# Language-model tower on one core: place of the embedding gathers on GpSimd, and the queue that issues the rows of all maxima

## The chip, the cores and the metric

The kernel runs on one core of a Trainium2 chip. The metric is the device time of one execution in microseconds, median of several. Engines are TensorE (PE), VectorE (DVE), ScalarE (ACT), GpSimd (POOL) and SyncE (SP); SPq in a profile row is SP's sequencer issuing DMAs.

## What is computed

```python
h = embeddings[x]                                  # x: 8 batches x 256 tokens, embeddings 8000 x 256, all float32
n = layernorm(h)
q, k, v = heads(n @ w_qkv)                         # 16 heads of 16
q, k = rotary(q), rotary(k)
h = h + (softmax(q @ k.T / 4) @ v).merge_heads() @ w_proj
n = layernorm(h)
e = argmax(n @ gate_w.T)                           # one of 8 experts per token
out = h + n + n @ expert_w[e].T
```

## The kernel before, in words

The work is cut into 8 batches (`NB`) of 256 tokens, each as two tiles (`NT`) of 128 rows. Each engine has its own program, written out by hand: a prologue, then `steps(step)`, which runs steps b = -1 to 9 of 16 slots s each. In step b TensorE computes for batch b the scores a second time, now turned and with the maximum already taken off (tile `t_pair`, `t_scores_tile`), ScalarE turns them into `probs` (`exp`), and TensorE multiplies those with the values into `o_bank`. In the same step the scores of batch b+1 are computed for the first time (tile `s_pair`, `scores_tile`), and VectorE takes their row maxima (`neg_max`, L857). So step -1 holds only first scores of batch 0, and step 0 is the first with second scores. Beside these the steps hold the front of a later batch (layer norm, QKV product, rotation, transposes, value product) by the tables `FRONT`, `EARLY`, `ONE` and `TWO`, the rest of attention of batch b-1 (`POST`), and the eight experts of batch b-2 in `e_bank`.

Exact float32 products come from float32r pairs: a high part, copied by ScalarE (`qk_high`, `x_high`, ...), and a low part, made by VectorE (`qk_low`, L849, and others).

Three things matter for the change.

**Gathers.** `gather(b)` on GpSimd issues two indirect DMAs (L325), each fetching 128 embedding rows into `h0` for one tile. VectorE's `f_norm_a(b)` (BN_STATS on `h0`, L811) waits for `gathered[b]`. GpSimd then computes the reciprocal deviation (`f_rs_of`, L335 and L337), VectorE normalizes (`xn`, L823), and TensorE transposes `xn` (L438) into the QKV product. In the prologue of GpSimd `gather(2)` stands behind the two rotation sums of batch 0 (`rotated_sum`, tile `qk`, L342), which wait for products of batch 0. `gather(3)` ends the prologue, and `gather(4)` to `gather(7)` stand at slot 6 of steps -1 and 0, where nothing else of GpSimd lies between.

**Restacking.** `restack(b)` on SP moves the rotated, transposed q and k parts into the operand layout `stacks`: six DMAs of 256 KB from SBUF to SBUF (L280). TensorE's first scores of batch b wait for all of them (`stack_in`).

**Rows of all maxima.** When the maxima of eight heads of a batch are complete, VectorE splits them (L864, L866), TensorE transposes them (L502), ScalarE copies the 16 rows to `max_rows` (`max_row`, L696), and SP issues two DMAs of 8 KB (`maximum(b, u)`, L267) which put them as two more operand rows into `stacks`. The second scores wait for them (`m_in[u]`, at v = 0 and v = 4). SP's order in a step is: maxima (b, 1), restack of b+2, maxima (b+1, 0), store of b-2. Each waits in order.

Of the kernel before, what the change touches and what calls it, by code (L numbers as in the profile page):

```python
# [7 lines left out]
F32 = mybir.dt.float32  # L8
# [12 lines left out]
STACKS = 3  # L21
# [14 lines left out]
def tower(nc, x, emb, w_qkv, w_proj, gate_w, expert_w, rope, ramp, out):  # L36
# [12 lines left out]
    with ExitStack() as ctx:  # L49
# [197 lines left out]
        @block.sync  # L247
        def _(sp):
            sp.sem_inc(out_ok, 16)
            sp.dma_start(ids[:, :], x).then_inc(ids_in, 16)  # L250
            for c in range(C):
                sp.dma_start(wqkv_raw[:, c, :], w_qkv[c * P:(c + 1) * P, :]).then_inc(wqkv_in[c], 16)
            sp.dma_start(rope_sb[:, :, :, :], rope).then_inc(rope_in, 16)
            sp.dma_start(ramp_sb[:, :], ramp).then_inc(rope_in, 16)
            sp.dma_start(gw_raw[:, :, :], gate_w).then_inc(gw_in, 16)

            for b in range(2):
                sp.wait_ge(gathered[b], 16 * NT)
            sp.dma_start(wp_raw, w_proj.rearrange("(c p) n -> p c n", p=P)).then_inc(wp_in, 16)
            sp.dma_start(ew_raw[:, :, :], expert_w).then_inc(ew_in, 16)  # L260

            def maximum(b, u):

                wait(sp, mt_ok, b * 2 + u + 1)
                for half in range(2):
                    r = 64 * half + KS
                    sp.dma_start(stacks[b % STACKS][r:r + 2, 4 * u:4 * u + 4, 0, :].bitcast(F32),  # L267
                                 max_rows[8 * half:8 * half + 8, u, :].bitcast(F32)).then_inc(m_in[u], 16)

            def restack(b):  # L270

                wait(sp, qkh_ok, b * NT + NT)
                wait(sp, t_ps, (b - STACKS) * NH + NH)
                for i in range(3):
                    if i == 1:
                        wait(sp, again_ok, b * NT + NT)
                        wait(sp, qkl_ok, b * NT + NT)
                    for half in range(2):
                        r = 64 * half
                        sp.dma_start(stacks[b % STACKS][r + i:r + KS:3, :, :, :].bitcast(F32).rearrange("d j k n -> d j (k n)"),  # L280
                                     parts[:, half, 2 * i:2 * i + 2, :].bitcast(F32)).then_inc(stack_in, 16)

            def store(b):
                wait(sp, res_ok, b + 2)
                sp.dma_start(out[b].rearrange("(t p) d -> p t d", p=P), res[:, :, :]).then_inc(out_ok, 16)

            def step(b, p):
                if here(b, 0):
                    maximum(b, 1)
                if here(b, 2):  # L290
                    restack(b + 2)
                if here(b, 1):
                    maximum(b + 1, 0)
                if here(b, -2):
                    store(b - 2)


            sp.wait_ge(ones_ok, 1)
            def ones_rows(i):
                for half in range(2):  # L300
                    r = 64 * half + KS
                    sp.dma_start(stacks[i][r:r + 2, :, 1, :].bitcast(F32), ones[:, :]).then_inc(ones_in, 16)

            for i in range(STACKS):
                ones_rows(i)
            restack(0)
            steps(step)
            sp.wait_ge(out_ok, 16 * (NB + 1))


        @block.gpsimd
        def _(pool):
# [61 lines left out]
            def step(b, p):  # L374
                for s in range(SLOTS):
                    g_at = SLOTS * b + s
                    for t in range(NT):
                        for k in batches(front, f"rotate{t}", g_at):
                            rotated_sum(k, t)
                    for k in batches(front, "stats", g_at):  # L380
                        f_rs_of(k)
                    for k in batches(post, "stats", g_at):
                        g_rs_of(k)
                    for k in batches(post, "g_norm", g_at):
                        residuals(k)
                    if s == 0 and here(b, -3):
                        finish(b - 3)
                    if s == 6 and b in (-1, 0):
                        gather(2 * b + 6)
                        gather(2 * b + 7)  # L390
                    if s % 2 and b == 1:
                        expert_weights([s // 2])
                if b == NB + 1:
                    finish(b - 2)
# [2 lines left out]
                gather_tile(j)  # L397
            f_rs_of(0)
            gather_tile(3)
            f_rs_of(1)  # L400
            rotated_sum(0, 0)
            rotated_sum(0, 1)
            gather(2)
            f_rs_of(2)
            rotated_sum(1, 0)
            rotated_sum(1, 1)
            gate_weights()
            rotated_sum(2, 0)
            rotated_sum(2, 1)
            gather(3)  # L410
            steps(step)


# [280 lines left out]
        def _(act):  # L694
# [22 lines left out]
            def max_row(b, u):  # L717
                wait(act, mt_ps, b * 2 + u + 1)
                copy(max_rows[:, u, :], o_bank[0:16, N:2 * N]).then_inc(mt_ok, 1)

            def exp(b, v):
                if v % 2 == 0:
# [331 lines left out]
```

## Time and profile before

| quantity | value |
|---|---|
| time, median of 3 runs | 328.38 us (328.08 to 330.29) |
| time of the profiled execution | 331.04 us |
| its span, first to last instruction | 329.2 us |
| busy share of the span | TensorE 86%, VectorE 74%, ScalarE 39%, GpSimd 26% |
| one step in the middle (step 3) | 33.5 us |
| prologue and step -1 together, until the first second scores | 58.7 us |

A timeline row has start and duration in us, then engine, line, operation, tiles, and in brackets how long the engine sat idle before and what ended that. A row of "windows" has the stretch and its length, then the busy time of each engine with its number of instructions, the granted TensorE clock (1.00 is 2.4 GHz, 0.50 is 1.2 GHz), the share of time that the 16 DMA engines were busy, and GB/s.

### The profile page before, as it was taken

The page shows a single profiled execution, that of the slowest core. Times are in us where ns is not written, and L with a number is a line of the kernel's source. Part 1 is how long each engine was busy: PE and PEld are TensorE (multiplying, and loading weights), DVE is VectorE, ACT ScalarE, POOL GpSimd, SP SyncE. Part 2 cuts the span into 40 slices and gives each one's busy share as a digit, 9 for nine tenths or more (in the row PEclk, how much of TensorE's full clock was granted, in tenths as well). Part 3 has the DMA queues.
Part 4 walks back from the last instruction along what each step waited for, and adds up shares of the span by engine and source line. Part 5 has one row for each costly group of instructions (what it writes and reads, how often), then busy time and mean ns, then how long its engine had stood idle before and what let it go on. Part 6 is the DMA issues. An engine that isn't in the chain of part 4 may idle for free.

```text
span 329.2 us, 5465 instructions
## 1 busy us (share of the span) xinstructions
PE 282.2 (86%) x2000; PEld 202.1 (61%) x2000; DVE 243.6 (74%) x595; ACT 126.9 (39%) x261; POOL 85.1 (26%) x96
## 2 busy tenths in 40 slices
PE   0384866789788899998999899989999999999894
PEld 0263744545565577667766677667666766667582
DVE  5764477565789887988798779877887985557763
ACT  3041030633596354435443544354454353431100
POOL 4551476011257601231122112220210120120311
PEclk9999675555999999999999999999999999999999
DMA  3269059093048029002900191019200000000000
GB/s 113 68 248 181 10 98 138 0 144 53 1 82 115 2 54 141 5 0 59 157 16 1 44 166 22 0 36 162 35 32 4 0 4 34 3 1 34 0 32 32
DMA packets 11590, 19.14 MB, mean 58 GB/s; under 512 B 2012, under 2 KB 4903, under 8 KB 11436
## 3 DMA queue, kind: packets, MB, share of 16 engines
q1 hardware_dynamic: 10796, 18.24, 29.1%
q0 software_dynamic: 768, 0.55, 1.2%
q8 instruction: 16, 0.26, 0.4%
q14 instruction: 10, 0.08, 0.1%
HBM read 5.30 MB, written 2.10 MB: 22 GB/s over the span
## 4 chain that ended last, share of the span: by engine, by line
PE 46%; DVE 25%; issue 11%; POOL 7%; DMA 5%; ACT 3%; SPq 1%; POOLq 0%; DVEq 0%; ACTq 0%
PE e_bank L424 13%; PE o_bank L554 7%; PE f_bank L424 7%; DVE acc L936 5%; PE t_pair L519 5%; DVE neg_max L857 5%; POOL qk L342 4%; DMA h<-in_emb,ids 2%; PE s_pair L424 2%; DMA stacks<-max_rows 2%; PE m_bank L566 2%; PE m_bank L424 2%; POOL res L360 2%; PE s_pair L490 1%; DVE xn L823 1%
## 5 line engine op out<-in xcount | busy, mean ns | idle before, releaser
L726 ACT ACTIVATE probs<-t_pair 128x512 f32<-128x512 f32 x128 | 69.6, 596 | 95.3 <-PE t_pair L519 94.8
L857 DVE TENSOR_REDUCE neg_max<-s_pair 128x2 f32<-128x512 f32 x128 | 81.9, 682 | 17.0 <-PE s_pair L490 16.4
L490 PE MATMUL s_pair<-stacks 48*128 48x256 f32 x256 | 55.8, 343 | 3.6 <-DVE neg_max L857 3.3
L519 PE MATMUL t_pair<-stacks 50*128 50x256 f32 x256 | 50.1, 326 | 5.4 <-DMA stacks<-max_rows 3.7
L519 PEld LDWEIGHTS t_pair<-stacks 50*128 50x128 f32 x256 | 35.9, 201 | 28.1 <-issue 25.1
L424 PE MATMUL e_bank<-ew_h,y_h 128*128 128x512 f32 x92 | 40.4, 439 | 4.7 <-DVE acc L932 2.7
L490 PEld LDWEIGHTS s_pair<-stacks 48*128 48x128 f32 x256 | 40.0, 213 | 6.3 <-DVE neg_max L857 5.1
L554 PE MATMUL o_bank<-probs,vals 128*32 128x256 f32 x512 | 36.9, 408 | 1.2 <-ACT max_rows L696 1.2
L936 DVE SCALAR_TENSOR_TENSOR acc<-e_bank,mask,acc 128x256 f32<-128x256 f32 x66 | 28.8, 478 | 11.2 <-PE e_bank L424 10.7
L424 PE MATMUL e_bank<-ew_l,y_h 128*128 128x512 f32 x92 | 36.3, 395 | 0.0
L424 PE MATMUL e_bank<-ew_h,y_l 128*128 128x512 f32 x92 | 36.3, 395 | 0.0
L342 POOL TENSOR_TENSOR qk<-rope_a,rope_b 128x512 f32<-128x512 f32 x16 | 20.7, 1294 | 49.0 <-DVE rope_b L844 49.0
L424 PEld LDWEIGHTS e_bank<-ew_h,y_h 128*128 128x128 f32 x92 | 17.3, 188 | 12.0 <-DVE acc L936 3.9
L554 PEld LDWEIGHTS o_bank<-probs,vals 128*32 128x32 f32 x512 | 14.0, 113 | 14.9 <-issue 7.5
L424 PE MATMUL f_bank<-wqkv_h,x_h 128*128 128x512 f32 (+1 forms) x44 | 17.7, 402 | 3.5 <-DVE x_l L828 2.6
L424 PEld LDWEIGHTS e_bank<-ew_l,y_h 128*128 128x128 f32 x92 | 17.3, 188 | 4.2
L335 POOL TENSOR_SCALAR f_ve<-f_mv 128x2 f32<-128x2 f32 x8 | 2.4, 295 | 67.3 <-DVE f_mv L814 67.3
L349 POOL TENSOR_SCALAR g_ve<-g_mv 128x2 f32<-128x2 f32 x8 | 2.0, 246 | 68.0 <-DVE g_mv L814 68.0
L696 ACT ACTIVATE o_t<-o_bank 128x256 f32<-128x256 f32 x32 | 12.5, 390 | 16.1 <-PE o_bank L554 16.1
L424 PEld LDWEIGHTS e_bank<-ew_h,y_l 128*128 128x128 f32 x92 | 17.4, 189 | 2.1
L325 POOL DMA_INDIRECT h<-in_emb,ids x16 | 16.8, 1048 | 6.1 <-issue 3.9
L360 POOL TENSOR_TENSOR res<-acc 128x512 f32<-128x512 f32 x8 | 10.2, 1276 | 31.0 <-DVE acc L936 31.0
(132 smaller groups left out, 529.8 us busy)
## 6 DMA issues: line engine op xcount, KB each, us to landing
stacks<-parts SPq DMA_DIRECT2D x48, 256.0 KB
ew_raw<-in_expert_w SPq DMA_DIRECT2D x1, 2048.0 KB, 9.2
out<-res SPq DMA_DIRECT2D x8, 256.0 KB, 2.1
probs<-in_w_qkv SPq DMA_DIRECT2D x2, 384.0 KB, 3.5
stacks<-max_rows SPq DMA_DIRECT2D x32, 8.0 KB
h<-in_emb,ids POOLq DMA_INDIRECT x16, 4.7
probs<-in_w_proj SPq DMA_DIRECT2D x1, 256.0 KB, 2.8
stacks<-ones SPq DMA_DIRECT2D x6, 16.0 KB
```

Source lines behind the costliest of these rows:

```text
L325: g.indirect_dma_start(h0[:, j, :], None, emb, bass.IndirectOffsetOnAxis(ap=ids[:, j:j + 1], axis=0), bounds_check=V - 1, oob_is_err=False ...
L342: g.tensor_tensor(qk[:, t, :, :, :].rearrange("p g d j -> p g j d"), rope_a[:, t, :, :].rearrange("p (g j) d -> p g j d", j=8), rope_b[:, ...
L360: g.tensor_tensor(res[:, :, :], acc[:, 0, :, :], acc[:, 1, :, :], ALU.add).then_inc(res_ok, 1)
L424: m = mm(o, a(c), w(c), start=(n == 0), stop=(n == 3 * C - 1))
L490: m = mm(s_pair[:, half, t * N:(t + 1) * N], stacks[b % STACKS][r:r + KS, pair, 0, t * P:(t + 1) * P], stacks[b % STACKS][r:r + KS, pair, ...
L519: m = mm(t_pair[:, half, c * N:(c + 1) * N], stacks[b % STACKS][r:r + KM, pair, 1, c * P:(c + 1) * P], stacks[b % STACKS][r:r + KM, pair, ...
L554: m = mm(o_bank[STRIP * j:STRIP * (j + 1), 0:N], vals[b % VALS][:, c, head(4 * g + j), :], probs[:, (4 * g + j) % RING, c, :], start=(c == ...
L566: m = tr(strips_bank(b, t)[:, g * P:(g + 1) * P], o_t[:, g, t * P:(t + 1) * P], ident[:, :])
L696: return nc.scalar.activation(o, i, ACT.Copy)
L726: nc.scalar.activation(probs[:, (2 * v + half) % RING, :, :].rearrange("p c n -> p (c n)"), t_pair[:, half, :], ACT.Exp, scale=SCALE).then ...
L857: v.tensor_reduce(neg_max[:, k // 4, :, 4 * half + k % 4], s_pair[:, half, :].rearrange("p (t n) -> p t n", t=NT), AX.X, ALU.max, negate=T ...
L936: v.scalar_tensor_tensor(out=acc[:, j, t, :], in0=y, scalar=mask[:, p, t, e:e + 1], in1=base[:, t, :] if u == 0 else acc[:, j, t, :], op0= ...
```

## The change

On GpSimd, `gather(2)` is issued right behind `gather_tile(3)` in the prologue, ahead of `f_rs_of(1)` and of the rotation sums of batch 0. `gather(3)` to `gather(7)` are issued one per step, at slot 1 of steps 0 to 4. The function `maximum` of SP is gone; its two DMAs are issued by ScalarE at the end of `max_row`, behind a wait for the copy that writes their source.

```diff
--- SP
-            def maximum(b, u):
-                wait(sp, mt_ok, b * 2 + u + 1)
-                for half in range(2):
-                    r = 64 * half + KS
-                    sp.dma_start(stacks[b % STACKS][r:r + 2, 4 * u:4 * u + 4, 0, :].bitcast(F32),
-                                 max_rows[8 * half:8 * half + 8, u, :].bitcast(F32)).then_inc(m_in[u], 16)
             def step(b, p):
-                if here(b, 0):
-                    maximum(b, 1)
                 if here(b, 2):
                     restack(b + 2)
-                if here(b, 1):
-                    maximum(b + 1, 0)
                 if here(b, -2):
                     store(b - 2)
--- POOL
-                    if s == 6 and b in (-1, 0):
-                        gather(2 * b + 6)
-                        gather(2 * b + 7)
+                    if s == 1 and b >= 0 and here(b, 3):
+                        gather(b + 3)
...
             gather_tile(3)
+            gather(2)
             f_rs_of(1)
             rotated_sum(0, 0)
             rotated_sum(0, 1)
-            gather(2)
             f_rs_of(2)
...
             rotated_sum(2, 1)
-            gather(3)
             steps(step)
--- ACT
             def max_row(b, u):
                 wait(act, mt_ps, b * 2 + u + 1)
                 copy(max_rows[:, u, :], o_bank[0:16, N:2 * N]).then_inc(mt_ok, 1)
+                wait(act, mt_ok, b * 2 + u + 1)
+                for half in range(2):
+                    r = 64 * half + KS
+                    act.dma_start(stacks[b % STACKS][r:r + 2, 4 * u:4 * u + 4, 0, :].bitcast(F32),
+                                  max_rows[8 * half:8 * half + 8, u, :].bitcast(F32)).then_inc(m_in[u], 16)
```

GpSimd's program from the first gathers on, before the change (L325 is a gather of one tile, L335 and L337 the deviation, L342 a rotation sum, L371 the gate weights, L366 expert weights):

```order
L325 DMA h<-in_emb,ids 128x256 x3
L335 TENSOR_SCALAR f_ve<-f_mv 128x2
L337 TENSOR_TENSOR f_rs<-f_ve,neg_half 128x2
L325 DMA h<-in_emb,ids 128x256
L335 TENSOR_SCALAR f_ve<-f_mv 128x2
L337 TENSOR_TENSOR f_rs<-f_ve,neg_half 128x2
L342 TENSOR_TENSOR qk<-rope_a,rope_b 128x4x8x16 x2
L325 DMA h<-in_emb,ids 128x256 x2
L335 TENSOR_SCALAR f_ve<-f_mv 128x2
L337 TENSOR_TENSOR f_rs<-f_ve,neg_half 128x2
```

The same place after the change (a gather is now L313, the deviation L323 and L325, a rotation sum L330):

```order
L313 DMA h<-in_emb,ids 128x256 x3
L323 TENSOR_SCALAR f_ve<-f_mv 128x2
L325 TENSOR_TENSOR f_rs<-f_ve,neg_half 128x2
L313 DMA h<-in_emb,ids 128x256 x3
L323 TENSOR_SCALAR f_ve<-f_mv 128x2
L325 TENSOR_TENSOR f_rs<-f_ve,neg_half 128x2
L330 TENSOR_TENSOR qk<-rope_a,rope_b 128x4x8x16 x2
L323 TENSOR_SCALAR f_ve<-f_mv 128x2
L325 TENSOR_TENSOR f_rs<-f_ve,neg_half 128x2
```

The two gathers of batch 2 have moved up past the deviation of batch 1 and both rotation sums of batch 0. Behind the last rotation sum of the prologue ten gathers in a row (batches 3 to 7) have become two (batch 3).

ScalarE's program in step 3, from the copy of the transposed q and k high part of tile 0, before (L726 is the exponential, L696 every copy):

```order
L696 ACTIVATE parts<-f_bank 128x2x2x128
L726 ACTIVATE probs<-t_pair 128x512 x2
L696 ACTIVATE parts<-parts 128x2x2x128
L696 ACTIVATE max_rows<-o_bank 16x256
L696 ACTIVATE parts<-f_bank 128x2x2x128
L726 ACTIVATE probs<-t_pair 128x512 x2
```

The same place after (copies are L682, exponentials L717, the DMAs L709):

```order
L682 ACTIVATE parts<-f_bank 128x2x2x128
L717 ACTIVATE probs<-t_pair 128x512 x2
L682 ACTIVATE parts<-parts 128x2x2x128
L682 ACTIVATE max_rows<-o_bank 16x256
L709 DMA stacks<-max_rows 2x4x256 x2
L682 ACTIVATE parts<-f_bank 128x2x2x128
L717 ACTIVATE probs<-t_pair 128x512 x2
```

Two DMA issues stand behind each of the 16 copies of maxima. On SP the 32 issues are gone, so that the restack of a batch no longer stands behind the maxima of the step.

## Rows read from the trace of the kernel before

**Rows 1.** The page: TensorE's granted clock in 40 slices, 8.2 us each

```profile
PEclk9999675555999999999999999999999999999999
```

**Rows 2.** The page: the chain that ended last, shares of the span by line

```profile
PE e_bank L424 13%; PE o_bank L554 7%; PE f_bank L424 7%; DVE acc L936 5%; PE t_pair L519 5%; DVE neg_max L857 5%; POOL qk L342 4%; DMA h<-in_emb,ids 2%; PE s_pair L424 2%; DMA stacks<-max_rows 2%; PE m_bank L566 2%; PE m_bank L424 2%; POOL res L360 2%; PE s_pair L490 1%; DVE xn L823 1%
```

**Rows 3.** Windows: steps 1 and 3

```profile
83.00:116.50 33.50, 28.05 (x251) 19.17 (x251) 28.53 (x66) 21.45 (x46) 17.17 (x16) 1.00 0.32 49
...
150.20:183.70 33.50, 32.22 (x251) 23.51 (x251) 28.49 (x73) 14.72 (x32) 7.05 (x8) 1.00 0.32 58
```

**Rows 4.** Timeline of GpSimd: the gather of tile 3, the gathers of batch 2

```profile
11.05 1.27 POOL L325 DMA_INDIRECT h<-in_emb,ids  x1 [0.19 <-issue]
15.20 0.22 POOL L335 TENSOR_SCALAR f_ve<-f_mv 128x2 f32<-128x2 f32 x1 [2.88 <-DVE f_mv L814]
...
21.78 1.14 POOL L325 DMA_INDIRECT h<-in_emb,ids  x1 [0.15 <-issue]
23.22 1.00 POOL L325 DMA_INDIRECT h<-in_emb,ids  x1 [0.30 <-issue]
```

**Rows 5.** Timeline of VectorE: moments of batch 1, low weights, statistics of batch 2

```profile
14.80 0.30 DVE L814 BATCH_NORM_AGGREGATE f_mv<-f_st 128x2 f32<-128x6 f32 x2
...
24.62 0.69 DVE L941 TENSOR_TENSOR wp_l<-probs,wp_h 128x512 fp32r<-128x512 f32 x1 [0.63 <-issue]
28.32 0.75 DVE L811 BATCH_NORM_STATS2 f_st<-h 128x6 f32<-128x256 f32 x2 [3.00 <-DMA h<-in_emb,ids]
```

**Rows 6.** Timeline of TensorE: transpose of batch 2

```profile
31.32 1.05 PE L438 MATMUL m_bank<-ident,xn 128*128 128x128 f32 x4 [3.57 <-DVE xn L823]
```

**Rows 7.** Windows of one microsecond: DMA after the expert weights, clock at 31 us

```profile
21.00:22.00 1.00, 0.47 (x5) 0.26 (x4) 0.09 (x1) 0.73 (x3) 0.85 (x2) 1.00 0.22 82
...
31.00:32.00 1.00, 0.68 (x4) 0.67 (x4) 1.00 (x3) 0.00 (x0) 0.00 (x0) 0.69 1.08 180
```

**Rows 8.** The chain: six products of batch 2, at half and at full clock

```profile
36.21 2.37 PE f_bank L424 x6
38.58 1.40 PE e_bank L424 x6
```

**Rows 9.** Windows: the restacks of batches 1, 2 and 3 in flight

```profile
45.00:57.00 12.00, 8.57 (x27) 6.10 (x26) 9.59 (x19) 0.37 (x1) 8.25 (x9) 0.50 1.09 155
...
67.00:77.00 10.00, 8.65 (x62) 5.36 (x54) 6.36 (x16) 5.21 (x12) 0.94 (x2) 0.50 1.03 158
...
95.00:105.00 10.00, 7.84 (x77) 5.62 (x74) 9.41 (x25) 7.49 (x16) 6.35 (x9) 1.00 1.02 157
```

**Rows 10.** The chain at the end of step -1, and TensorE's first second score

```profile
51.70 6.64 DMA stacks<-max_rows
...
58.69 0.55 PE L519 MATMUL t_pair<-stacks 50*128 50x256 f32 x1 [3.66 <-DMA stacks<-max_rows]
```

**Rows 11.** Timeline of VectorE: the last maxima of batch 0

```profile
54.48 1.29 DVE L857 TENSOR_REDUCE neg_max<-s_pair 128x2 f32<-128x512 f32 x2 [0.29 <-PE s_pair L490]
```

**Rows 12.** Line L267: duration in ns (min/median/max), first and last start

```profile
L267 SPq DMA_DIRECT2D stacks<-max_rows x32: 610/616/664, 51.0 to 274.8; - x32
```

**Rows 13.** The page: DMA issues of the output store, median us to landing

```profile
out<-res SPq DMA_DIRECT2D x8, 256.0 KB, 2.1
```

**Rows 14.** Timeline of ScalarE around the copy of maxima, steps 1 and 3

```profile
92.28 0.36 ACT L696 ACTIVATE max_rows<-o_bank 16x256 fp32r<-16x256 f32 x1
92.91 0.60 ACT L696 ACTIVATE vals<-f_bank 128x512 f32<-128x512 f32 x1 [0.27 <-PE f_bank L424]
...
96.83 0.62 ACT L696 ACTIVATE o_h<-m_bank 128x512 fp32r<-128x512 f32 x1
...
152.91 0.60 ACT L696 ACTIVATE parts<-f_bank 128x512 fp32r<-128x512 f32 x1
```

**Rows 15.** Step 3: VectorE's low part of tile 1, TensorE's value product

```profile
153.54 0.69 DVE L849 TENSOR_TENSOR parts<-f_bank,parts 128x512 fp32r<-128x512 f32 x1
...
155.37 0.28 PE L424 MATMUL f_bank<-wqkv_h,x_h 128*128 128x256 f32 x1
```

## The prediction

> **What bounds the kernel now.** I read the page first. TensorE's granted clock is full except in a stretch of slices near 33 us and from about 41 to 82 us [rows 1]. The chain that ended last is mostly TensorE and VectorE work, but it holds two DMA entries of 2% each, the gather into `h` and the rows of all maxima; 2% of 329.2 us is 6.6 us for each [rows 2]. Then I read windows by step. Step 3 has TensorE busy 32.22 of 33.5 us: there it is the bound and only about 1.3 us are free. Step 1 has 28.05 of 33.5 us, because expert work has not begun; it is bound by a chain over several engines and has ScalarE at 21.45 us instead of 14.72 us, since it also splits the expert weights there [rows 3]. Last I looked at the two places where a DMA entry of the chain becomes idle time. In the prologue VectorE sits idle for 3.00 us until the gather of batch 2 lands at 28.3 us, and TensorE then waits 3.57 us for the normalized batch 2 [rows 5, 6]. At the start of step 0 TensorE waits 3.66 us for the rows of all maxima of batch 0, whose DMA is in flight for 6.64 us, until 58.34 us [rows 10]. Nothing else of the two topics shows as a wait on the path, so the change can give only at these two places, plus what the granted clock adds.
>
> **Gather of batch 2, earlier.** It is issued at 21.78 and 23.22 us now, behind two rotation sums. In the new order it follows the gather of tile 3, which ends at 11.05 + 1.27 = 12.32 us. Two issues at the durations and gaps of the present pair (0.15 + 1.14 + 0.30 + 1.00 = 2.59 us) end at 14.9 us [rows 4]. The next GpSimd instruction, the deviation of batch 1, waits until 15.1 us for VectorE's moments in any case (14.80 + 0.30) [rows 5] and stands idle for 2.88 us before it [rows 4]. So the two issues lie in that hole and cost nothing; if they took 0.5 us longer, the excess would fall on batch 1 alone, which has its own slack behind batch 0. The landing: the last gather was issued at 23.22 us and landed at 28.3 us, 5.1 us later, in company of the first restack. Now the expert weights are in flight beside it, and the DMA engines have fallen to a share of 0.22 by 21 to 22 us [rows 7], so it has landed by 22 us at the latest. VectorE reaches its statistics only behind the low part of the projection weights, which ends at 24.62 + 0.69, overlapped to about 25.25 us [rows 5]. Gain: 28.32 - 25.25 = 3.05 us. All behind it (deviation, `xn`, transposes, the rotation of batch 1, the product of batch 2) hangs on this one instruction in VectorE's order and moves up by the same amount. VectorE's own order is late next, not the DMA. Bounds: 3.05 us if the weights stay where they are; 2.5 us if the two issues delay batch 1's path a little.
>
> TensorE's idle time ahead of this transpose shrinks from 3.57 to 0.5 us, and a second, shorter hole behind it, the wait for the rotation sum of batch 1, stays. The granted clock fell to 0.69 at 31 us and then to 0.50, behind the 3.57 us hole [rows 7]. If it stayed full, the six products of batch 2 behind it would be about 1.0 us shorter (2.37 us against 1.40 us for six at either clock [rows 8]). But it is reduced again from the slice of 41 to 49 us on [rows 1], where TensorE has no hole as long as that one, so I count this at zero and keep 1.0 us for the range.
>
> **Later gathers, one per step.** The eight gathers of batches 4 to 7 leave the stretch in which the restack of batch 1 is in flight (45 to 57 us, in which GpSimd runs nine gathers in 8.25 us). With them that restack keeps the DMA engines busy for 12 us (45 to 57 us). The restacks of batches 2 and 3, same size, no gathers, need 10 us each [rows 9]. I take the difference, about 2.2 us since the two gathers of batch 3 stay: the restack lands near 55.0 us on the old time axis instead of 57.2 us, where the 12 us end. At their new places, slot 1 of a step, GpSimd has 17.17 and 7.05 us of work in 33.5 us [rows 3]; each pair costs 2.6 us there, is needed seven slots (some 14 us) later, and delays nothing but a first piece of expert weights in step 1, needed in step 2. Cost: nothing.
>
> **Rows of all maxima, on ScalarE's queue: what it brings.** ScalarE's copy is its only instruction between 45 and 57 us [rows 9], so it can issue when SP did, from 51.0 us [rows 12], ending at about 52.3 us. Until now the two DMAs queued behind 1.5 MB of restack on the same queue and landed 6.64 us after the issue [rows 10]. On another queue they are only beside it. Bounds for the landing: 2 us after the issue (2.1 us, the landing of a store [rows 13]) is 54.3 us; all the way behind the restack, which itself now lands at 55.0 us, is 56.1 us. I take 55.3 us. But the first visit of step 0 also waits for the restack of batch 1 (55.0 us) and for the maxima of batch 0, of which the first half is ready at 54.48 + 0.65 = 55.1 us and the rest at 54.48 + 1.29 = 55.8 us [rows 11]. So three waits end almost together, and TensorE starts at about 55.8 us instead of 58.69 us. Gain 2.9 us, between 2.1 (behind the restack) and 3.5 us (only the maxima left). What is late next is VectorE.
>
> The Trainium skill bears on this in two places. "Trainium Kernel Development and Optimization", section Key Constraints, says that DMAs of all queues share the same 16 engines and that a second issuer only saves the sequencer's issue time; by that the queue brings nothing, and this term would be the 2.2 us from the gathers alone, 0.7 us less. "DMA: Bandwidth & Descriptors", section on queues and rings, says that an engine takes turns between the queues that it has work for, by which the small rows pass the restack. The 6.64 us flight is what one shared queue looks like; no row here shows two hardware queues at once.
>
> **What it costs.** Sixteen copies are each followed by two issues that now stand in ScalarE's order. On SP one takes 616 ns [rows 12]; I take the same, so 2 x 0.64 + 0.05 = 1.3 us per copy, 21 us of ScalarE time in all. Not measured on ScalarE: the low bound is nothing, the high one 1.6 us. Most of it falls into waits for TensorE. Where not:
> - Step 1. ScalarE has 0.27 us of idle time behind the copy at 92.28 us, then runs values, expert weights, exponentials and `o_h` (96.83 us) with no gap worth the name [rows 14]. So `o_h` comes 1.3 - 0.3 = 1.0 us late, and the chain of step 1 runs through it (out projection, residual, norm). TensorE is not the bound there [rows 3], so the 1.0 us stays. The second copy of step 1 is followed by a wait for TensorE, and I cost it at nothing.
> - Steps 2 to 5. The high part of tile 1 follows the copy at once (152.91 us) [rows 14]. It moves to 154.2, the low part on VectorE from 153.54 to 154.8, ending 155.5, and TensorE's value product (155.37 us) waits for it [rows 15]: 0.2 us late. Four such steps at 0.1 to 0.2 us: 0.6 us. VectorE's order then carries 1.3 us, which it gives back in its next wait for TensorE: it is free for 5 of 33.5 us [rows 3].
> - The copy of the next batch's maxima at slot 11: exponentials and `y_h` come 1.3 us later, and their readers stand behind a whole expert product in TensorE's order, 1.4 us at full clock as six products of that size are [rows 8]. Nothing.
> Sum of costs 1.6 us, bounds 0 and 3.7 us (if the steps in the middle pay 0.7 us each).
>
> Taking SP out of the maxima lets the restack go a little earlier; it is not waited for in any step but 0, so nothing.
>
> **The sum.** -3.05 - 2.9 + 1.6 = -4.35 us. The profiled execution took 331.04 us (span 329.2 us and 1.84 us around it), so it would become 326.7 us. It was 2.66 us above the median of the runs; the same difference on the median gives 328.38 - 4.35 = 324.0 us.
>
> **Rivals.**
> - *The wait only changes its name.* The restack of batch 1 keeps 12 us of flight, because bandwidth inside SBUF, not the gathers, sets it (155 GB/s with gathers, 158 and 157 without [rows 9] would fit that). TensorE then waits for `stack_in` until about 57.9 us, gain 0.7 instead of 2.9 us: 326.2 us. Against it stands the recorded time, 2 us more at nearly the same rate. By the section Key Constraints named above the time would be 324.7 us.
> - *The clock.* With the prologue's hole gone and the one at 55 us gone, the granted clock stays or returns to full earlier. From 49 to 82 us it was at half [rows 1]. Keeping it in the prologue gives 1.0 us, a return 3 us earlier in step 0, where TensorE is busy for 8.65 of 10 us at that clock [rows 9], another 1.5 us: 321.5 us.
> - *ScalarE's queue becomes the bound.* The place is `max_row`: a stalled issue holds back exponentials, which hold back TensorE's second scores and the outputs. At 1.3 us in full for all 16 copies it is 20.8 us against a gain of 5.95 us: 328.38 + 14.9 = 343 us. It decides from 0.37 us of loss per copy on (5.95 / 16), and is slower by over 1% from 0.58 us on. For it: ScalarE must wait for its own copy each time, and the maxima sit in front of exponentials. Against it: ScalarE is idle for more than half of every step [rows 3].
> - *Not what it says.* A gather of batch 2 that lands after 25.25 us because of the expert weights; excluded by rows 7 but for an unknown.
>
> **Chances.** The forecast 0.50, with its own range 322.6 to 325.5 us. Clock 0.17. Wait renamed 0.13. ScalarE's cost at two to three times my figure, near 326 us, 0.13. ScalarE as the bound 0.07. A change of 1%, 3.3 us, is about what a measurement of this kernel can tell from none. Below 325.1 us lie most of the forecast and all of the clock case: 0.62. Within 1%: 0.31. Slower by over 1%: 0.07. The range goes from 320.5 us (-3.05, -3.5, no cost, clock 1.0, rounded) to 328.0 us (gains of 3.05 and 0.7, cost 3.7).
>
> **What would show it.** Right, if VectorE's statistics of batch 2 start near 25.25 us with no wait for a DMA; if the first second score starts 5 to 6.5 us earlier than 58.69 us, its wait ended by VectorE or by a DMA landing within half a microsecond of it; if the stretch of busy DMA engines of that restack is 10 us; if ScalarE's queue rows last about 0.6 us; if step 1 is some 1 us longer and step 3 at most 0.3 us. Wrong, if that first visit still waits for the restack, if steps 2 to 5 grow by over 0.7 us each, or if the granted clock has another shape.

## The result, and the profile after

The changed kernel takes 335.9 us, the median of 5 runs (334.23 to 336.18), against 328.4 us (328.08 to 330.29): ratio 1.020, 95% interval 1.0173 to 1.0228. It is slower by 7.5 us where 4.35 us of gain were forecast, and lies outside the range. The profiled execution took 334.23 us with a span of 332.4 us, 3.2 us more than the span of before. Executions of one kernel differ here by 2 to 6 us with their mean granted clock, so the ratios leave out executions of the slower kind where a kernel showed both (three of seven for gathers alone, four of nine for held until landed, one of eight for held until copied, four of ten for both queues), and the traces are compared place by place.

First the page of the changed kernel: the granted clock in 40 slices and the chain that ended last, by line.

```profile
PEclk9999765659798999999999999999999999999999
...
PE e_bank L410 14%; PE f_bank L410 6%; PE o_bank L540 6%; DMA stacks<-max_rows 6%; DVE acc L927 4%; PE t_pair L505 4%; DVE neg_max L848 4%; PE m_bank L410 3%; ACTq L709 3%; ACT parts L682 3%; POOL qk L330 2%; ACT probs L717 2%; PE s_pair L410 2%; PE s_pair L476 2%; POOL res L348 2%
```

The gather into `h` has left the chain [rows 2], as intended. The rows of all maxima have not: they have grown from 2% to 6%, and a new entry, ScalarE's queue (ACTq L709), has 3%. TensorE's waits, from the list of who waited for whom (total, times, longest), show the same:

```profile
PE t_pair L505 <- DMA stacks<-max_rows: 8.8, 3, 4.0
```

One wait of 3.66 us [rows 10] has become three. Where they stand, in TensorE's timeline of the changed kernel:

```profile
55.09 0.55 PE L505 MATMUL t_pair<-stacks 50*128 50x256 f32 x1 [2.13 <-DMA stacks<-max_rows]
...
68.88 0.58 PE L505 MATMUL t_pair<-stacks 50*128 50x256 f32 x1 [3.97 <-DMA stacks<-max_rows]
...
97.73 0.38 PE L505 MATMUL t_pair<-stacks 50*128 50x256 f32 x1 [2.70 <-DMA stacks<-max_rows]
```

The first is the old one: the first second score is at 55.09 instead of 58.69 us, 3.6 us earlier. The other two stand in front of the fifth pair of heads (v = 4) of steps 0 and 1, where no DMA was waited for before. They are for the rows of (b, 1), the second half of the heads.

A clock for the whole run are ScalarE's 16 copies of maxima (start in us; the last columns are the difference to before). The versions are those of the experiments below.

| copy of | before | changed | changed - before | gathers alone - before | held - before |
|---|---|---|---|---|---|
| (0, 0) | 50.59 | 48.52 | -2.07 | -2.26 | -2.45 |
| (0, 1) | 64.16 | 60.52 | -3.64 | -3.64 | -3.87 |
| (1, 0) | 71.04 | 70.74 | -0.30 | -3.65 | -3.87 |
| (1, 1) | 92.28 | 90.06 | -2.22 | -4.17 | -4.66 |
| (2, 0) | 100.08 | 101.31 | +1.23 | -4.17 | -2.45 |
| (2, 1) | 118.54 | 120.65 | +2.11 | -4.19 | -0.03 |
| (3, 1) | 152.47 | 154.56 | +2.09 | -4.18 | -0.02 |
| (4, 1) | 185.94 | 188.41 | +2.47 | -4.19 | +0.34 |
| (5, 1) | 219.41 | 222.24 | +2.83 | -4.19 | +0.69 |
| (7, 1) | 273.75 | 276.93 | +3.18 | -4.16 | +1.09 |

So the changed kernel is 3.64 us ahead until the copy of (0, 1). It loses 3.34 us at the first new wait and regains 1.92 us in step 0. In step 1 it loses 3.45 us up to the copy of (2, 0), a stretch that holds the second new wait but also two issues on ScalarE, and 0.88 us more behind that copy; then 3 x 0.36 us in steps 3 to 5. The sum is +3.19 us. The regain is clock: the granted clock is at full for slices of step 0 in which it was at half before [rows 1].

The prologue, in GpSimd's and VectorE's timelines, answers to [rows 4, 5]:

```profile
12.37 1.01 POOL L313 DMA_INDIRECT h<-in_emb,ids  x1 [0.30 <-issue]
13.68 1.01 POOL L313 DMA_INDIRECT h<-in_emb,ids  x1 [0.30 <-issue]
15.14 0.22 POOL L323 TENSOR_SCALAR f_ve<-f_mv 128x2 f32<-128x2 f32 x1 [0.45 <-DVE f_mv L805]
```

```profile
19.80 0.69 DVE L831 TENSOR_TENSOR rope_a<-e_bank,rope_sb 128x512 f32<-128x512 f32 x1 [1.20 <-PE e_bank L410]
...
25.55 0.69 DVE L932 TENSOR_TENSOR wp_l<-probs,wp_h 128x512 fp32r<-128x512 f32 x1 [0.46 <-ACT wp_h L682]
26.15 0.75 DVE L802 BATCH_NORM_STATS2 f_st<-h 128x6 f32<-128x256 f32 x2
```

Both gathers lie in GpSimd's hole, and the statistics of batch 2 follow the low weights at once, with no wait for a DMA. They start at 26.15 instead of 28.32 us.

The new mechanism is in SP's and ScalarE's queues. In step 0, from the chain (the flight is counted from the start of the second of the two issues):

```profile
60.91 0.62 ACTq L709
61.57 7.27 DMA stacks<-max_rows
68.84 0.04 issue
```

The rows of (0, 1) were in flight for 7.27 us. What was on the DMA engines then, queue by queue (packets, MB, share of 16 engines; q1 is SP's, q10 ScalarE's), in the stretches 60 to 62, 62 to 64, 64 to 66 and 66 to 68 us:

```profile
q1 hardware_dynamic: 197, 0.37, 84.6%
...
q1 hardware_dynamic: 157, 0.29, 105.9%
...
q1 hardware_dynamic: 159, 0.29, 100.0%
q10 hardware_dynamic: 10, 0.01, 3.8%
...
q1 hardware_dynamic: 173, 0.32, 102.5%
q10 hardware_dynamic: 10, 0.01, 3.9%
```

SP's queue is the restack of batch 2, 1.5 MB. SP began to issue it at 59.18 us, 1.7 us before the rows were issued. In the kernel before, SP issued the rows of (b, 1) first and could not reach the restack of b+2 until they were out. With the rows gone from SP, the restack starts as soon as its parts are ready, which in steps 0 and 1 is before the copy of (b, 1) (tables `TWO` and `EARLY`: transposes in slots 0 and 1, the copy in slot 3). The 20 packets of the rows then move 10 by 10, the first of them more than 3 us after their issue. From step 2 on the second transpose stands in slot 3 behind the copy, so the restack can't overtake, and no wait appears.

### The profile page after: what moved, and what is told of

The parts are those of the page before. It is cut to its first block, busy times and chain, and to the rows that moved or that the text cites. A ratio compares the mean times of both kernels' runs of the same rounds, so it can differ in the third digit from the quotient of the medians.

```text
span 332.4 us, 5465 instructions
## 1 busy us (share of the span) xinstructions
PE 282.8 (85%) x2000; PEld 201.8 (61%) x2000; DVE 244.0 (73%) x595; ACT 127.0 (38%) x261; POOL 85.5 (26%) x96
## 4 chain that ended last, share of the span: by engine, by line
PE 44%; DVE 20%; issue 11%; ACT 8%; DMA 7%; POOL 6%; ACTq 3%; POOLq 0%; DVEq 0%
PE e_bank L410 14%; PE f_bank L410 6%; PE o_bank L540 6%; DMA stacks<-max_rows 6%; DVE acc L927 4%; PE t_pair L505 4%; DVE neg_max L848 4%; PE m_bank L410 3%; ACTq L709 3%; ACT parts L682 3%; POOL qk L330 2%; ACT probs L717 2%; PE s_pair L410 2%; PE s_pair L476 2%; POOL res L348 2%
## 5 line engine op out<-in xcount | busy, mean ns | idle before, releaser
L717 ACT ACTIVATE probs<-t_pair 128x512 f32<-128x512 f32 x128 | 69.7, 597 | 95.1 <-PE t_pair L505 86.3
L330 POOL TENSOR_TENSOR qk<-rope_a,rope_b 128x512 f32<-128x512 f32 x16 | 20.6, 1293 | 50.8 <-DVE rope_b L835 50.8
L337 POOL TENSOR_SCALAR g_ve<-g_mv 128x2 f32<-128x2 f32 x8 | 2.0, 244 | 68.2 <-DVE g_mv L805 68.2
L323 POOL TENSOR_SCALAR f_ve<-f_mv 128x2 f32<-128x2 f32 x8 | 2.4, 297 | 66.1 <-DVE f_mv L805 66.1
L682 ACT ACTIVATE o_t<-o_bank 128x256 f32<-128x256 f32 x32 | 12.5, 390 | 16.8 <-PE o_bank L540 13.7
L313 POOL DMA_INDIRECT h<-in_emb,ids x16 | 17.1, 1070 | 5.5 <-issue 3.4
```

The costliest lines, as they stand in the source:

```text
L313: g.indirect_dma_start(h0[:, j, :], None, emb, bass.IndirectOffsetOnAxis(ap=ids[:, j:j + 1], axis=0), bounds_check=V - 1, oob_is_err=False ...
L330: g.tensor_tensor(qk[:, t, :, :, :].rearrange("p g d j -> p g j d"), rope_a[:, t, :, :].rearrange("p (g j) d -> p g j d", j=8), rope_b[:, ...
L682: return nc.scalar.activation(o, i, ACT.Copy)
L717: nc.scalar.activation(probs[:, (2 * v + half) % RING, :, :].rearrange("p c n -> p (c n)"), t_pair[:, half, :], ACT.Exp, scale=SCALE).then ...
```

## The experiments

Times are medians in us over all executions; "before" is the kernel before, run beside them.

| run | time | before | ratio to before (95%) |
|---|---|---|---|
| gathers alone | 322.9 | 328.95 | 0.978 (0.974 to 0.982) |
| the same again | 324.92 | 328.59 | 0.987 (0.9825 to 0.9916) |
| rows on ScalarE alone | 340.22 | 328.95 | 1.033 (1.0289 to 1.037) |
| changed, restack held until rows landed | 331.36 | 328.95 | 1.0001 (0.9955 to 1.0046) |
| changed, restack held until rows copied | 332.34 | 328.95 | 1.0092 (1.0057 to 1.0127) |
| gather of batch 2 alone | 326.15 | 329.52 | 0.9918 (0.9889 to 0.9946) |
| later gathers alone | 329.04 | 329.52 | 0.9981 (0.9951 to 1.0011) |
| held, issues one slot later | 326.28 | 329.52 | 0.9866 (0.979 to 0.9941) |
| rows on both queues | 327.44 | 329.52 | 0.9883 (0.9835 to 0.9931) |
| gathers, SP's order swapped | 368.37 | 328.59 | 1.1207 (1.1169 to 1.1245) |
| changed, issues one slot later, not held | 337.17 | 328.59 | 1.0232 (1.0176 to 1.0287) |

**Each half alone.** The first run keeps `maximum` on SP and takes only the gathers from the change.

```diff
             def step(b, p):
                 if here(b, 0):
                     maximum(b, 1)
                 if here(b, 2):
                     restack(b + 2)
                 if here(b, 1):
                     maximum(b + 1, 0)
```

> Both moves of the gathers, maxima still issued by SP in the old order. Theory (the restack overtakes the maxima rows only because SP no longer stands between them): the first second score starts near 55.1 us, no wait of TensorE for maxima rows at v = 4 of steps 0 and 1, steps 3 to 5 at 33.5 us; time 328.4 - 3.6 = about 324.8 us. Rival (the moved gathers bring a loss of their own in steps 0 and 1, for instance by meeting the restacks): the waits in front of the second scores of v = 4 appear here too and the time is 328 us or more.

TensorE's timeline of this version:

```profile
55.05 0.55 PE L517 MATMUL t_pair<-stacks 50*128 50x256 f32 x1 [2.29 <-DMA stacks<-max_rows]
```

That is the only wait for rows left in its timeline of TensorE. The lead of 3.64 us holds through step 0, grows by 0.5 us with the clock, and is 4.2 us to the end (table). The rival falls. The row says one thing more: the first second score comes at 55.05 us with the rows on SP's queue and at 55.09 us on ScalarE's. The own queue brought nothing there. The seven executions lie between 321.45 and 326.9 us, and the ratio of 0.978 comes from four at a mean granted clock of 0.957 or more, so it was run again.

> The version with the gather moves alone, once more in five rounds: 322 to 327 us depending on the granted clock in the first 100 us, ratio to the kernel before 0.98 to 0.99. The version with both repairs of ScalarE's issues should not differ from it by more than 1 us at the same granted clock.

The second time six executions of 322.92 to 327.4 us gave 0.987, which is the better figure for this version, since all six count in it.

The other half: gathers as before, rows on ScalarE.

```diff
                 copy(max_rows[:, u, :], o_bank[0:16, N:2 * N]).then_inc(mt_ok, 1)
+                wait(act, mt_ok, b * 2 + u + 1)
+                for half in range(2):
+                    r = 64 * half + KS
+                    act.dma_start(stacks[b % STACKS][r:r + 2, 4 * u:4 * u + 4, 0, :].bitcast(F32),
+                                  max_rows[8 * half:8 * half + 8, u, :].bitcast(F32)).then_inc(m_in[u], 16)
```

> Only the issue of the maxima rows moved to ScalarE, gathers as before. Theory: first second score hardly earlier than 58.69 us (0 to 0.7 us), then the two waits for maxima rows of the changed kernel (3.3 and 3.5 us of lost lead), less what the granted clock gives back in step 0, 0.9 us in step 1 and 3 x 0.36 us in steps 3 to 5; time 334 to 337 us. Rival (the two edits meet badly and neither is bad alone): 328 to 330 us.

TensorE's timeline, steps 0 and 1:

```profile
72.69 0.58 PE L507 MATMUL t_pair<-stacks 50*128 50x256 f32 x1 [5.00 <-DMA stacks<-max_rows]
...
103.22 0.38 PE L507 MATMUL t_pair<-stacks 50*128 50x256 f32 x1 [2.82 <-DMA stacks<-max_rows]
```

340.22 us, more than the 334 to 337 us expected; the first new wait is 5.00 us here instead of 3.97 us. The first second score starts at 58.90 us, no earlier than the 58.69 us of before, so the own queue brings nothing at that place here either. This half is the loss: 11 us by itself, less some 4 to 6 us of gain by the gathers.

**Splitting the gathers.** First only `gather(2)` is moved up, against the kernel before:

```diff
             gather_tile(3)
+            gather(2)
             f_rs_of(1)
             rotated_sum(0, 0)
             rotated_sum(0, 1)
-            gather(2)
```

> Only gather of batch 2 moved up. Theory: the low weights and the statistics of batch 2 follow each other on VectorE near 26 us, everything behind is 2.1 to 3 us earlier, the first second score near 56.5 us with its wait for the maxima rows still there: 326 us beside 328.4 to 329. Rival (the wait at step 0 swallows it, since it is set by something that does not move): first second score still near 58.7 us, no gain.

Then only the later gathers:

```diff
-                    if s == 6 and b in (-1, 0):
-                        gather(2 * b + 6)
-                        gather(2 * b + 7)
+                    if s == 1 and b >= 0 and here(b, 3):
+                        gather(b + 3)
...
             rotated_sum(2, 1)
-            gather(3)
```

> Only the later gathers spread over steps 0 to 4. Theory: the restack of batch 1 keeps the DMA engines busy for 10 instead of 12 us, first second score 1.5 to 2 us earlier than 58.69 us, 327 us beside 328.4 to 329. Rival (bandwidth inside SBUF sets the restack, whatever the gathers do): 12 us of DMA and no gain.

The first gives 0.9918 and its first second score at 56.50 us. The second gives 0.9981, not told from no change, though the first second score is 1.2 us earlier (57.48 us); the stretch of busy DMA engines is 10 to 11 us long, from 45 to 56 us. In the windows of this run (columns as in [rows 9], the DMA engines' share last but one):

```profile
46.00:56.00 10.00, 8.42 (x26) 5.96 (x26) 8.45 (x16) 0.37 (x1) 0.00 (x0) 0.50 1.00 140
56.00:57.00 1.00, 0.00 (x0) 0.00 (x0) 0.30 (x2) 0.00 (x0) 0.00 (x0) 0.50 0.04 4
```

With nine gathers beside it, it was 12 us [rows 9]. Queue by queue, though, the difference is hardly the restack. In the kernel before, 248 of the 270 packets between 56 and 58 us are those of GpSimd's gathers. SP's queue, with restack and rows together, had 27 of its 884 packets left at 55.5 us there and has 16 left here, after a start at 43.7 and 43.85 us. So the gathers lengthened the stretch of busy DMA engines, and their packets stood beside those of the rows, which land 1.2 us earlier without them (57.13 instead of 58.34 us). The restack itself was less than 1 us longer with them. Where the rows have their own queue its packets can be told apart: with the gathers (rows on ScalarE alone) they begin near 45.0 us and 8 of 864 are left at 56.0 us; without (the changed kernel) they begin near 42.9 us and 9 are left at 53.0 us. The rival's time is refuted, since TensorE starts 1.2 us earlier; its premise, that the gathers do not set the restack's flight, is nearer to these rows than the 2 us of the theory.

**Holding the restack back.** Two ways to give SP its old order on top of the changed kernel, once until the rows have landed and once until they are copied.

```diff
                 if here(b, 2):
+                    if here(b, 0):
+                        wait(sp, m_in[1], b * 32 + 32)
                     restack(b + 2)
```

> The changed kernel, but SP issues the restack of batch b+2 only after the maxima rows of (b, 1) have landed. Theory: both waits at v = 4 vanish, the flight of those rows is about 2 us after their issue, the lead of 3.6 us over the kernel before holds until step 1; what is left is ScalarE's cost of 2 us: 326.5 to 327 us. Rival (ScalarE's own issue time makes the waits): TensorE still waits 2 us or more at both places and the time stays above 333 us. The restacks start 2 to 5 us later and are not waited for.

```diff
                 if here(b, 2):
+                    if here(b, 0):
+                        wait(sp, mt_ok, b * 2 + 2)
                     restack(b + 2)
```

> As the run before, but SP waits only for the copy of the maxima, so that restack and maxima rows are issued at the same moment on two queues. If the order of issue is all that counts: 326.5 to 327 us, no waits. If small rows on their own queue are slowed by any restack in flight beside them: flight of 3 to 6 us and a wait of 1 to 3 us at v = 4 in steps 0 and 1, 328 to 333 us.

Held until landing, both waits at v = 4 are gone. The rows are issued at 60.68 us for 1.28 us, and SP's first restack DMA starts at 63.26 us, which is their landing: 1.3 us after the end of the issues, and 1.9 us after the start of the second one. ScalarE's queue and SP's in its timeline:

```profile
60.68 1.28 ACTq L711 DMA_DIRECT2D stacks<-max_rows  x2
```

```profile
63.26 3.78 SPq L272 DMA_DIRECT2D stacks<-parts  x6
```

Held until the copy only, with rows and restack issued at the same moment, the rows fly 5.88 us and TensorE waits again, as its timeline shows:

```profile
66.98 0.58 PE L507 MATMUL t_pair<-stacks 50*128 50x256 f32 x1 [2.46 <-DMA stacks<-max_rows]
...
95.14 0.38 PE L507 MATMUL t_pair<-stacks 50*128 50x256 f32 x1 [1.93 <-DMA stacks<-max_rows]
```

The wait is thus set by the restack in flight beside the rows, and not by ScalarE's issue. Holding is worth 4.5 us in the medians (335.9 to 331.36 us). But the held version takes 331.36 us, not 326.5 to 327: here my theory was too small in its second term. The table shows where. Up to (1, 1) it is level with the gathers alone. From (1, 1) to (2, 0) it takes 10.01 us against 7.80, from (2, 0) to (2, 1) 20.88 against 18.44, and steps 3 to 5 cost 0.36 us each. ScalarE's issues cost 2.2 + 2.4 + 1.1 = 5.7 us. This also corrects the reading of step 1 in the changed kernel: from the copy of (1, 1) to that of (2, 1) the changed kernel takes 30.59 us and the held one 30.89 us, where the gathers alone take 26.24 us. With ScalarE's issues in place the second new wait of the changed kernel thus costs nothing that these traces can tell; its time is lost in the held version too, in other waits and at a lower clock. In the traces, the order of restack and rows costs the changed kernel the 3.34 us of the first wait, less the clock that comes back after it.

**Is it ScalarE's place or ScalarE's time?** The held version with the issues moved behind the work that follows the copies.

```diff
             def max_row(b, u):
                 wait(act, mt_ps, b * 2 + u + 1)
                 copy(max_rows[:, u, :], o_bank[0:16, N:2 * N]).then_inc(mt_ok, 1)
-                wait(act, mt_ok, b * 2 + u + 1)
-                for half in range(2):
...
+            def issue_rows(b, u):
+                wait(act, mt_ok, b * 2 + u + 1)
+                for half in range(2):
...
                     if b == 1 and s % 2:
                         expert_weights(s // 2)
+                    if here(b, 0) and s == 4:
+                        issue_rows(b, 1)
+                    if here(b, 1) and s == (9 if maxima_slot(b + 1) == 9 else 12):
+                        issue_rows(b + 1, 0)
```

> As the held version (restack of b+2 behind the landing of the maxima rows), but ScalarE issues the rows one slot later: those of (b, 1) at the end of slot 4 behind the exponentials and the high part, those of (b+1, 0) at the end of slot 9 or 12. Theory (the issues cost what they hold back behind the copy: high part, low part, value product; in step 1 expert weights, GpSimd's deviation and the norm): steps 3 to 5 come back to 33.5 us (1.1 us in all) and most of the 4.6 us in step 1 goes, 326 to 328 us where the held version stood at 331.4. Rival (1.3 us of ScalarE's time is lost wherever it stands): within 1 us of the held version.

326.28 us. Its copies of (1, 1), (2, 0) and (2, 1) are 7.80 and 18.44 us apart, the same as with the gathers alone, and its last one at 268.96 us stands 4.79 us ahead of before. All of ScalarE's cost is gone, although it issues the same 32 DMAs. At a granted clock of 0.937 to 0.940 it takes 326.3 to 326.6 us and the gathers alone 326.5 to 327.4 us: less than 1 us apart.

Then both queues: on top of the gathers alone, the rows of (b+1, 0) go on ScalarE right behind the copy, those of (b, 1) stay on SP ahead of the restack.

```diff
             def step(b, p):
                 if here(b, 0):
                     maximum(b, 1)
                 if here(b, 2):
                     restack(b + 2)
-                if here(b, 1):
-                    maximum(b + 1, 0)
...
                 copy(max_rows[:, u, :], o_bank[0:16, N:2 * N]).then_inc(mt_ok, 1)
+                if u == 0:
+                    wait(act, mt_ok, b * 2 + u + 1)
+                    for half in range(2):
...
```

> Both gather moves; maxima rows of (b, 1) from SP ahead of the restack as before, those of (b+1, 0) from ScalarE. Theory: no wait for rows at v = 4, first second score at 55.1 us as with SP's queue alone, so ScalarE's queue brings nothing there; ScalarE's 1.3 us behind the copy of (2, 0) in step 1 costs about 2 us (expert weights, then GpSimd, then the norm), the copies at slot 11 nothing: 2 us over the version with the gather moves alone, 325 us. Rival (the own queue helps the first visit): first second score at 54.5 us or earlier and a time at or below 322.9 us.

327.44 us, where 325 us were expected. The first second score starts at 53.94 us, which by itself looks like the rival (54.5 us or earlier). But the copy of (0, 0) also stands earlier here, at 47.32 instead of 48.33 us, before its rows were issued: from that copy to the first second score it is 6.62 us here, 6.57 us in the changed kernel, and 6.72 and 6.79 us in the two runs of gathers alone. So the own queue is worth some 0.2 us at most at this place. There is no wait at v = 4, and it is 7.81 us from (1, 1) to (2, 0), but 20.90 us from (2, 0) to (2, 1): the issue behind the copy of (2, 0) costs 2.46 us alone, and steps 3 to 5 are back at 33.5 us, so the copies at slot 11 cost nothing.

**One repair, and the order on one queue.** The version with the issues one slot later, without the hold:

```diff
                 if here(b, 2):
-                    if here(b, 0):
-                        wait(sp, m_in[1], b * 32 + 32)
                     restack(b + 2)
```

> The changed kernel with ScalarE's issues one slot later and SP not held. Theory (two separate terms): the wait for rows at v = 4 of steps 0 and 1 is as in the changed kernel or 1 to 2 us longer, ScalarE's term of 5 us is gone: 330 to 333 us beside 329.5, between the changed kernel (335.9) and the version with both repairs (326.3). Rival (one repair is enough): 327 us or less.

337.17 us, where 330 to 333 us were expected: no better than the changed kernel. The rows are issued at 61.88 us instead of 60.91 us, behind the same restack, and the waits at v = 4 are 6.85 and 5.40 us. Steps 3 to 5 are back at 33.5 us, so ScalarE's cost there is gone, but the longer waits take more than the whole of it. The two repairs do not add: the hold alone is worth 4.5 us, the later issue alone nothing, and both together 9.6 us (medians, each against the 335.9 us of the changed kernel).

Last, the gathers alone with SP's first two pieces of a step swapped:

```diff
-                if here(b, 0):
-                    maximum(b, 1)
                 if here(b, 2):
                     restack(b + 2)
+                if here(b, 0):
+                    maximum(b, 1)
```

> Both gather moves, all issues on SP as before, but the restack of b+2 now stands ahead of the maxima rows of (b, 1) in SP's order. Theory (the order of restack and rows is what costs in steps 0 and 1, whatever queue the rows are on): the rows of (0, 1) queue behind 1.5 MB, TensorE waits 4 to 6 us at v = 4 of step 0 and some 3 us in step 1; steps 3 to 5 stay at 33.5 us; 329 to 332 us, 5 us or more over the version with the gather moves alone. Rival (the wait of the changed kernel came from the second queue itself): no wait at v = 4, 323 to 327 us.

TensorE's timeline of step 0:

```profile
71.49 0.58 PE L517 MATMUL t_pair<-stacks 50*128 50x256 f32 x1 [6.96 <-DMA stacks<-max_rows]
```

368.37 us, far more than expected. Behind the restack on one queue the wait is 6.96 us in step 0 and 6.28 in step 1, and it comes in the later steps too, because SP now stands in the restack's own waits before it issues the rows. I had left those steps out, so the 368.37 us do not measure the order in steps 0 and 1 alone. The waits there confirm that order is what counts, with either queue.

## Why the prediction was wrong, point by point

**The step that failed** is the sentence "Taking SP out of the maxima lets the restack go a little earlier; it is not waited for in any step but 0, so nothing." I asked who waits for the restack, and not what it would collide with. Starting it a few microseconds earlier puts 1.5 MB on the DMA engines ahead of two DMAs of 8 KB that TensorE needs 4 us after their issue (issued at 60.91 us, idle from 64.91 us). Held back, both waits vanish, and the time falls by 4.5 us. In the changed kernel the first wait costs 3.34 us of lead; the second can't be told from ScalarE's cost in the same stretch. The second step that failed is ScalarE's cost, put at 1.6 us, which is about as large an error (below).

**ScalarE's queue brings something: no.** I put the landing at 55.3 us on the old axis, between "2 us after the issue" and "behind the restack", and the gain at 2.9 us. Shifted by the prologue, the rows landed at 54.71 us, about 1.5 us after the restack's last packets (53.2 us), so the gain was 3.6 - 2.1 = 1.5 us (2.1 us of lead were there at the copy of (0, 0) already), below my lower bound of 2.1. I had taken the end of the busy DMA engines for the landing of the restack, and all 12 us of them for the restack, where the last of them were packets of gathers. With SP's queue the start is the same to 0.04 us. The rule of the Trainium skill, "Trainium Kernel Development and Optimization", section Key Constraints, that a second issuer saves only issue time, agrees with these rows; I had given it the smaller weight. That engines take turns between queues (the Trainium skill, "DMA: Bandwidth & Descriptors", section Queues, rings and completion order) is not contradicted, since the rows' packets move between those of the restack; but a flight of 1.9 us became one of 5.9 to 7.3 us all the same. Whether the turns themselves are the cause no run here shows.

**ScalarE's cost** I summed to 1.6 us; it is 5.7 us in the held version. One issue takes 620 ns, as assumed from SP [rows 12]; in what the trace tells of this one line of the changed kernel (durations in ns, min, median and max):

```profile
L709 ACTq DMA_DIRECT2D stacks<-max_rows x32: 620/621/1246, 48.9 to 278.0; - x32
```

The misses are the places. Behind the copy of (1, 1) I had 1.0 us and it is 2.2; behind that of (2, 0) I had nothing and it is 2.4; steps 2 to 5 had 0.6 and took 1.1. The chain of the held version shows the second:

```profile
98.69 0.62 ACTq L711
...
99.36 0.64 ACT ew_h L684
...
100.07 1.27 POOL ew_l L356
101.33 0.20 POOL g_ve L339
101.60 0.72 POOL g_rs L341
102.32 0.03 issue
102.35 0.74 DVE yn L890 x2
...
103.14 0.65 PE m_bank L578 x4
103.79 2.44 PE f_bank L412 x6
```

I had looked only at what ScalarE's next wait hides. The copy of expert weights behind the issue feeds a subtraction on GpSimd, which works in order, and behind that stands the deviation that VectorE's norm waits for. And the six products at the end take 2.44 us instead of 1.6: TensorE waited 1.46 us for the norm, and the clock was granted at half right after. The same happened behind the copy of (1, 1), where the twelve products of the out projection take 2.7 us in the held version (94.48 to the next product at 97.20 us) against 1.5 us with gathers alone (94.06 to 95.59 us). Somewhat less than half of the two terms is clock, read from those two groups (1.2 and 0.8 us of 2.2 and 2.4 us). I had let the clock only give.

**The gathers: right in mechanism.** The two issues lie in GpSimd's hole, no DMA is waited for, the DMA engines are busy for 10 us, and later gathers cost nothing. The term of 3.05 us measured 2.2 us (28.32 - 26.15). The low weights stood at 25.55 instead of 24.62 us, because TensorE's products of batch 0 came 0.43 us apart for longer: they went over to 0.24 us near 18 us before, and stayed at 0.43 us up to 19.6 us here (VectorE waits 1.20 us for `e_bank` at 19.8 us, where it had 0.29 us before). That is nearly the pace of products at half clock [rows 8], but the granted clock reads 1.00 in both traces there, so these runs leave open why. Alone, the gathers bring 4.2 us in the trace and 0.987 of the time when repeated: near the 4.35 us that I gave to the whole change.

**The rival on the other side** had the right place, but its price rested on ScalarE alone. At 5.7 us over 16 copies it came to 0.36 us each, just under the 0.37 us from which it decides. The held version shows that cost without the waits: 331.36 us, beside 328.95 us, which takes back the whole gain and at most 2.4 us more. The rest, up to 335.9 us, was the order of two transfers, which no rival named.

**Sums.** 28.32 - 25.25 is 3.07 and not 3.05 us, and the ends of the range add up to 320.8 and 328.3 us, where I wrote 320.5 and 328.0 us. None of it matters beside the terms above.

## What to carry to other kernels

A queue's order can act as a priority: before an issue is moved away from it, look at what stood behind it and now starts earlier, and whose bytes that meets. A small transfer that something waits for belongs ahead of a large one, and putting it on another queue does not replace that. An issue moved to a compute engine costs its time for whatever stands behind it, over other in-order engines too; one slot later the same issue can be free.

## What the runs showed that I had not expected

- Two DMAs of 8 KB land 1.9 us after the start of the second issue with idle DMA engines, and 5.9 to 7.3 us after it beside a transfer of 1.5 MB on another queue.
- A small hole can cost more than its length: in step 1 of the held version, idle times of TensorE of 0.94 and 1.46 us were each followed by a stretch at 1.2 GHz, while with gathers alone one of 0.66 us at the same place was not. The clock also gives back: the changed kernel, with a wait of 4 us in step 0, regained 1.9 us there through full clock. Why the clock returned earlier is not settled by these runs.
- The best version found is the gathers alone (0.987 and 0.978 in two series), level with both repairs on ScalarE's queue (0.987). No run beat it.
